# Experts' outputs transposed, from gated and split silu values, with all weights split ahead by GpSimd

## The reference, cut to what matters

```python
x = x + tanh(g_xattn) * attention(layernorm(x), ctx)      # 16 heads of 64, causal: the first 56 keys count
xf = layernorm(x).reshape(448, 128)
gates = softmax(xf @ router_w)                            # 14 routed experts, the best 2 kept
masked = gates of the best 2 / (their sum + 1e-9)
h_e = rmsnorm(xf) * rms_w[e]                              # per expert
routed = sum over e of masked[:, e] * (silu(h_e @ W1[e]) @ W2[e])   # W1 128x256, W2 256x128
shared = sum over 2 shared experts of silu(h @ W1) @ W2
x = x + tanh(g_ffn) * (routed + shared)
```

## Time and profile before

| what | us |
|---|---|
| median of 3 runs | 117.86 (117.8 to 119.21) |
| the profiled execution, its own time | 117.94 |
| its span (first to last instruction) | 116.1 |
| PE busy | 107.2 (92%) |
| PE weight loads busy | 91.6 (79%) |
| DVE busy | 69.3 (60%) |
| ACT busy | 59.4 (51%) |
| POOL busy | 43.8 (38%) |

### The profile page before, as it was taken

The page is one execution under the profiler, slowest core; times in us unless marked ns, Lnnn a source line. Parts: engine busy times, 40 slices in busy tenths (PEclk is TensorE's granted clock), DMA queues, the critical chain, the costliest instruction groups (busy, mean ns, idle before and its releaser), DMA issues.

```text
span 116.1 us, 2394 instructions
## 1 busy us (share of the span) xinstructions
PE 107.2 (92%) x826; PEld 91.6 (79%) x826; DVE 69.3 (60%) x195; ACT 59.4 (51%) x99; POOL 43.8 (38%) x75
## 2 busy tenths in 40 slices
PE   6699999996999999999699999999999999999980
PEld 6687768745496487488489989999999999999970
DVE  0068966659688789879843329999333333333360
ACT  5053787943579579579964298333333333333300
POOL 7803599000001000100101798666666666663000
PEclk9999999999999999999999999999999999999999
DMA  3899999999997000000000000000000000000003
GB/s 90 254 295 285 416 413 413 420 420 444 421 428 308 28 0 0 0 6 0 0 0 6 0 6 0 3 3 0 0 6 0 0 0 0 0 0 0 0 0 79
DMA packets 3169, 13.76 MB, mean 119 GB/s; under 512 B 431, under 2 KB 1007, under 8 KB 2775
## 3 DMA queue, kind: packets, MB, share of 16 engines
q1 hardware_dynamic: 3159, 13.63, 31.3%
HBM read 13.40 MB, written 0.23 MB: 117 GB/s over the span
## 4 chain that ended last, share of the span: by engine, by line
PE 57%; DVE 14%; DMA 12%; ACT 8%; SPq 4%; issue 3%; DVEq 0%; ACTq 0%
PE score_ps L736 15%; DMA ctx_all<-in_ctx_dram 12%; PE attn_ps L736 8%; PE ring L729 6%; PE ring L731 6%; PE ring L730 6%; PE ring L597 5%; ACT square_junk L816 4%; PE score_ps L552 4%; PE attn_ps L621 3%; DVE probs L1046 3%; DVE row_sum L1039 2%; DVE row_max L1025 2%; DVE probs L1032 2%; PE score_ps L546 2%
## 5 line engine op out<-in xcount | busy, mean ns | idle before, releaser
L938 ACT ACTIVATE mixT<-ring 128x896 f32<-128x896 f32 x16 | 14.6, 917 | 26.9 <-PE ring L731 26.9
L736 PE MATMUL score_ps<-w,mixT 128*112 (+1 forms) x160 | 19.1, 273 | 0.2 <-ACT mixT L938 0.2
L736 PEld LDWEIGHTS score_ps<-w,mixT 128*112 128x112 f32 x160 | 18.7, 177 | 0.8 <-issue 0.3
L437 POOL TENSOR_TENSOR h_scale<-h_base,minus_half 112x1 f32<-112x1 f32 x4 | 2.2, 547 | 41.7 <-DVE h_base L1069 41.7
L1210 DVE SCALAR_TENSOR_TENSOR xn_rows<-score_ps,gates,xn_rows 112x128 f32<-112x128 f32 x36 | 10.1, 343 | 11.5 <-PE score_ps L736 11.3
L621 PEld LDWEIGHTS attn_ps<-wkq_space,mixT 128*112 128x112 f32 x128 | 14.2, 177 | 2.4 <-issue 2.4
L621 PE MATMUL attn_ps<-wkq_space,mixT 128*112 128x128 f32 x128 | 15.0, 276 | 0.0
L402 POOL TENSOR_TENSOR w_full<-w,columns 128x256 f32 (+1 forms) x16 | 9.8, 612 | 11.5 <-PE ring L731 10.5
L729 PE MATMUL ring<-hT_hi,w_hi 128*128 128x448 f32 (+2 forms) x36 | 13.9, 386 | 0.1
L731 PE MATMUL ring<-hT_hi,w_lo 128*128 128x448 f32 (+2 forms) x36 | 12.6, 350 | 0.0
L730 PE MATMUL ring<-hT_lo,w_hi 128*128 128x448 f32 (+2 forms) x36 | 12.6, 349 | 0.0
(11 more groups left out here) (136 smaller groups left out, 186.7 us busy)
## 6 DMA issues: line engine op xcount, KB each, us to landing
ctx_all<-in_ctx_dram SPq DMA_DIRECT2D x4, 1500.0 KB, 18.8
w<-in_w_dram SPq DMA_DIRECT2D x2, 1792.0 KB, 27.3
wkq_space<-in_wkq_dram SPq DMA_DIRECT2D x2, 512.0 KB, 6.1
wvo<-in_wvo_dram SPq DMA_DIRECT2D x1, 1024.0 KB, 10.6
w<-in_w_shared_dram SPq DMA_DIRECT2D x2, 256.0 KB, 16.4
ctx_head<-in_ctx_head_dram SPq DMA_DIRECT2D x1, 480.0 KB, 8.9
ctx_headT<-in_ctx_headT_dram SPq DMA_DIRECT2D x1, 224.0 KB, 4.9
x_space<-in_x_rows_dram SPq DMA_DIRECT2D x1, 224.0 KB, 5.7
```

The source lines that it names most:

```text
L736: last = nc.tensor.matmul(dst, hidden[slot][:, c, t * ROWS:(t + 1) * ROWS], w2_chunk(c), start=(c == 0), stop=(c == 1))
L938: nc.scalar.activation(hidden[slot], ring[:, 2 * slot:2 * slot + 2, 0:TOKENS], ACT.Silu).then_inc(S["hidden_ready"], 1)
```

## The change

Outputs of experts are made with tokens along the columns (128 x 448), in one PSUM bank that sums over all experts, `out_sums`. So a gate is no longer one number per partition: DVE multiplies the hidden values (2 x 448 columns) by a tile that holds the gate of each token in all 128 rows (`gate_hidden`). The tiles of the first three routed experts are made by PE (`spread_gates`) from the transposed gates, split in hi and lo; those of the other eleven go through DRAM and come back by DMA, spread over the partitions. Experts 0 to 3 are multiplied by W2 in plain float32 (`output_whole`, two products of 448 columns); 4 to 15 from split values (`output_parted`, six fp32r products): ACT rounds the gated values (`round_hidden`), DVE subtracts (`subtract_hidden`). The shared experts' W2 is multiplied by tanh(g) beforehand. The loop is written out, and PE runs up to 5 experts ahead with the hidden products. The last expert is summed apart, in two halves of columns, and added by DVE; the result leaves transposed, in two DMAs, and is turned back on the host.

POOL splits all of W1, and W2 of experts 4 to 15, into places that hold them for good, most of it in the attention stage, with the four `second_scale` steps (the former L437) between. To make room, weights are loaded in fours into buffers that the attention has done with (`stages`), the context has room for two loads instead of four, and SP waits on semaphores between its loads. POOL also builds the matrix that spreads the gates.

```diff
+WHOLE = [0, 1, 2, 3]
+PARTED = [e for e in range(EXPERTS) if e not in WHOLE]
+FULL_SLOTS = 8
...
+GATE_GROUPS = [(3, 4), (4, 5), (5, 7), (7, ROUTED)]
+GATE_ROWS = 32
+CTX_SLOTS = 4
+AHEAD = 6
...
+        w1_hi, w1_lo = (sb(n, [P, EXPERTS, HIDDEN], FP32R) for n in ("w1_hi", "w1_lo"))
+        w2_hi, w2_lo = (sb(n, [P, len(PARTED), 2, D], FP32R) for n in ("w2_hi", "w2_lo"))
+        w2_whole = sb("w2_whole", [P, len(WHOLE), 2, D])
...
+        hidden_slots = key_space.rearrange("p (s c n) -> p s c n", s=FULL_SLOTS, c=2)
+        hi_slots = (parts(A_hi[:, :, :].rearrange("p h d -> p (h d)"), 2)
+                    + parts(ctx_hi_space, 1) + parts(probs_hi_space, 1))
+        lo_slots = (parts(A_lo[:, :, :].rearrange("p h d -> p (h d)"), 2)
+                    + parts(ctx_lo_space, 1) + parts(probs_lo_space, 1))
...
+                if 2 * n >= CTX_SLOTS:
+                    sp.wait_ge(S["squares_done"], GROUPS + 2 * n + 2 - CTX_SLOTS)
...
+            context(0)
+            context(1)
+            sp.dma_start(w2_whole[:, 0:SHARED, :, :], A["w2_shared"]).then_inc(S["w2_shared_loaded"], 16)
+            sp.dma_start(w2_whole[:, SHARED:, :, :], A["w2"][:, 0:len(WHOLE) - SHARED, :, :])\
+                .then_inc(S["w2_whole_loaded"], 16)
+            sp.wait_ge(S["ctx_lo_ready"], 1)
+            first_four(0)
+            sp.wait_ge(S["w1_scaled_ready"], SHARED)
+            sp.dma_start(stage_pair[:, :], A["w1"][:, 6 - SHARED:8 - SHARED, :].rearrange("p e f -> p (e f)"))\
+                .then_inc(S["w1_pair_loaded"], 16)
+            wait_filled(sp, "M3")
+            first_four(1)
+            first_four(2)
+            context(2)
+            sp.wait_ge(S["w1_scaled_ready"], 6)
+            second_four(0)
+            context(3)
+            sp.wait_ge(S["w1_scaled_ready"], 12)
+            second_four(1)
+            sp.wait_ge(S["w1_scaled_ready"], EXPERTS)
+            second_four(2)
+            sp.wait_ge(S["gatesT_ready"], 1)
+            sp.dma_start(gates_dram, gatesT).then_inc(S["gates_stored"], 16)
+            sp.wait_ge(S["gates_stored"], 16)
+            for n, (a, z) in enumerate(GATE_GROUPS):
+                sp.dma_start(gate_tiles[:, a - SPREAD:z - SPREAD, :], gates_dram[a:z, :].partition_broadcast(P))\
+                    .then_inc(gates_loaded[n], 16)
...
-                    .then_inc(S["w1_hi_ready"], 1)
-                pool.wait_ge(S["w1_hi_ready"], e + 1)
-                pool.wait_ge(S["w1_full_ready"], e + 1)
-                nc.gpsimd.tensor_tensor(w1_lo[slot][:, :], w1_full[:, :],
-                                        w1_hi[slot][:, :].bitcast(FP32), ALU.subtract)\
-                    .then_inc(S["w1_scaled_ready"], 1)
-            def scale_w1_static(e):
...
+                    nc.gpsimd.tensor_tensor(w1_full[:, :], first_weights(e),
+                                            rms_cols[:, e:e + 1].to_broadcast([P, HIDDEN]), ALU.mult)\
+                        .then_inc(S["w1_full_ready"], 1)
+                    pool.wait_ge(S["w1_full_ready"], e + 1)
+                    nc.gpsimd.tensor_copy(w1_hi[:, e, :], w1_full[:, :])\
+                        .then_inc(S["w1_hi_ready"], 1)
+                    pool.wait_ge(S["w1_hi_ready"], e + 1)
+                    nc.gpsimd.tensor_tensor(w1_lo[:, e, :], w1_full[:, :],
+                                            w1_hi[:, e, :].bitcast(FP32), ALU.subtract)\
+                        .then_inc(S["w1_scaled_ready"], 1)
...
+                    nc.gpsimd.tensor_copy(w2_hi[:, n, :, :], weights)\
+                        .then_inc(S["w2_hi_ready"], 1)
+                    pool.wait_ge(S["w2_hi_ready"], n + 1)
+                    nc.gpsimd.tensor_tensor(w2_lo[:, n, :, :], weights,
+                                            w2_hi[:, n, :, :].bitcast(FP32), ALU.subtract)\
+                        .then_inc(S["w2_split_ready"], 1)
...
+            split_w1(range(6))
...
+            split_w1(range(6, 12))
+            second_scale(0)
+            split_w1(range(12, EXPERTS))
+            second_scale(1)
+            split_w2(range(4, 8))
+            pool.wait_ge(S["tanh_ready"], 1)
+            pool.wait_ge(S["w2_shared_loaded"], 16)
+            nc.gpsimd.tensor_tensor(w2_whole[:, 0:SHARED, :, :], w2_whole[:, 0:SHARED, :, :],
+                                    tanh_col[:, 1:2].unsqueeze(2).unsqueeze(3)
+                                    .to_broadcast([P, SHARED, 2, D]), ALU.mult)\
+                .then_inc(S["w2_shared_scaled"], 1)
+            second_scale(2)
+            split_w2(range(8, 12))
+            second_scale(PAIRS - 1)
...
+            pool.wait_ge(S["logits_ready"], 1)
+            split_w2(range(12, 14))
+            pool.wait_ge(S["gatesT_ready"], 1)
+            split_w2(range(14, EXPERTS))
...
+            def next_hidden(e):
+                pe.wait_ge(S["hidden_ready"], e - 1)
+                hidden_products(e).then_inc(S["hidden_filled"], 1)
+            def output_whole(e):
+                if e < SHARED:
+                    pe.wait_ge(S["w2_shared_scaled"], 1)
+                    pe.wait_ge(S["hidden_ready"], e + 1)
...
+                    pe.wait_ge(S["hidden_gated"], e - SHARED + 1)
                 for c in range(2):
-                    last = nc.tensor.matmul(dst, hidden[slot][:, c, t * ROWS:(t + 1) * ROWS],
-                                            w2_chunk(c), start=(c == 0), stop=(c == 1))
+                    last = nc.tensor.matmul(out_sums, w2_whole[:, WHOLE.index(e), c, :], hidden(e)[:, c, :],
+                                            start=(e == 0 and c == 0), stop=False)
+                last.then_inc(S["expert_done"], 1)
+            def output_parted(e, sums, cols=slice(0, TOKENS)):
+                n = PARTED.index(e)
+                hi, lo = (hidden_part(slots, e) for slots in (hi_slots, lo_slots))
+                pe.wait_ge(S["w2_split_ready"], n + 1)
+                pe.wait_ge(S["hidden_hi_ready"], n + 1)
+                alone = e == EXPERTS - 1
+                for c in range(2):
+                    nc.tensor.matmul(sums, w2_hi[:, n, c, :], hi[:, c, cols],
+                                     start=(alone and c == 0), stop=False)
+                    nc.tensor.matmul(sums, w2_lo[:, n, c, :], hi[:, c, cols],
+                                     start=False, stop=False)
+                pe.wait_ge(S["hidden_lo_ready"], n + 1)
+                for c in range(2):
+                    last = nc.tensor.matmul(sums, w2_hi[:, n, c, :], lo[:, c, cols],
...
+            next_hidden(2)
+            output_whole(0)
+            next_hidden(3)
+            output_whole(1)
...
+            next_hidden(4)
+            pe.wait_ge(S["gates_ready"], 1)
+            for t in range(PAIRS):
+                last = nc.tensor.transpose(gatesT_ps[:, t * ROWS:(t + 1) * ROWS], gates[:, t, :],
+                                           ident[0:ROWS, 0:ROWS])
+            last.then_inc(S["gatesT_filled"], 1)
+            next_hidden(5)
+            def spread_gates(n):
+                nc.tensor.matmul(gate_banks[n], spread[:, n, :], gates_parts, start=True, stop=True)\
...
+            for e in range(3, EXPERTS - 1):
+                if e in WHOLE:
+                    output_whole(e)
+                else:
+                    output_parted(e, out_sums).then_inc(S["expert_done"], 1)
+                if e + AHEAD - 1 < EXPERTS:
+                    next_hidden(e + AHEAD - 1)
+            for n, cols in enumerate(halves):
+                output_parted(EXPERTS - 1, last_sums[n], cols).then_inc(S["half_done"], 1)
...
+                n = PARTED.index(e)
+                act.wait_ge(S["hidden_gated"], e - SHARED + 1)
+                if n >= PART_SLOTS:
+                    act.wait_ge(S["expert_done"], PARTED[n - PART_SLOTS] + 1)
+                nc.scalar.activation(hidden_part(hi_slots, e), hidden(e), ACT.Copy)\
+                    .then_inc(S["hidden_hi_ready"], 1)
...
+            for e in range(2):
+                silu(e)
+            act.wait_ge(S["logits_ready"], 1)
+            nc.scalar.activation(expo[:, :, :], shifted[:, :, :], ACT.Exp)\
...
+            nc.scalar.activation(x1T, x1T_ps, ACT.Copy).then_inc(S["x1T_ready"], 1)
+            silu(4)
+            act.wait_ge(S["gatesT_filled"], 1)
+            nc.scalar.activation(gates_parts, gatesT_ps, ACT.Copy).then_inc(S["gates_hi_ready"], 1)
+            act.wait_ge(S["w2_split_ready"], 4)
+            nc.scalar.activation(gatesT, gatesT_ps[0:ROUTED, :], ACT.Copy)\
+                .then_inc(S["gatesT_ready"], 1)
+            for e in range(5, 8):
+                silu(e)
+            round_hidden(4)
+            for e in range(8, EXPERTS):
+                round_hidden(e - 3)
+                silu(e)
+            for e in range(EXPERTS - 3, EXPERTS):
+                round_hidden(e)
...
-            def add_expert(place, gate, before=moe):
-                for t in range(PAIRS):
-                    last = nc.vector.scalar_tensor_tensor(
```

(23 more changed lines are left out.)

313 lines of the change are left out of this document (161 added, 152 removed).

## The result

The changed kernel takes 121.29 us (median of 4 runs, 120.56 to 122.08), the kernel before 117.83 beside it: a ratio of 1.029, 95% interval 1.020 to 1.038. It is slower. The profiled execution took 121.75 us, with a span of 119.9 against 116.1.

The account below looks back on a forecast made before the run. PE alone was taken to bound the expert stage, and a tight DVE, PE and ACT chain the attention stage. 117.94 - 5.1 (expert stage and end) + 8.4 (late POOL) = 121.2 us; range 116.5 to 124.5.

Parts of the forecast that it names:

- case A: Attention stage: POOL is late at h_scale and held up by DVE too; 121.2 us, range 119.5 to 123; chance 0.48.
- POOL's start after the load: POOL, attention stage: the next four experts' weights land at 25.6 us; from there POOL runs without a break.
- An expert's W1: POOL, attention stage: splitting one expert's W1 takes 1.9 us, with a copy put at 0.33.
- The spreading matrix: POOL, attention stage: memset, two selects and a copy take 2.2 us with waits, bounds 1.6 and 3.5.
- POOL's loss to DVE: Attention stage: POOL loses 0.5 us to each of seven L1046 instructions, 3.5 us up to the third h_scale.
- The waits are not to be added up: DVE's waits for h_scale: the third comes at 61.8 us when POOL's work is done, whatever DVE loses before.
- The loss by the clock after the first gap goes into the second wait: PE, attention stage: a clock fall after the first h_scale gap is absorbed by the wait at the third.
- C: Rival, attention stage: case A plus PE's clock falling in gaps ahead of h_scale, 2.5 us more, 123.7; chance 0.18.
- The fourth `h_scale` is covered: POOL, attention stage: it comes 4 x 1.1 + 0.6 us behind the third and is wanted about 7 us after it.
- The expert stage: From first expert output to last product: 39.3 us instead of 44.4, plus 1.0 charged for DVE; net gain 5.1.
- The end: After PE's last product: one DVE add of 224 columns, some 0.5 us with its wait; 1.05 less; output transfer unchanged.
- D: Rival, attention stage: POOL keeps up with DVE at h_scale, only the stage gain is left; 112.8 us; chance 0.10.

Follow-up runs that it names:

- inverse_in_psum: Changed kernel with the softmax inverse (row_inv) kept in PSUM and the idle products between the first transposes left out: 119.61 us, ratio 1.012.
- first_scale_early: Changed kernel with only POOL's first h_scale moved ahead of experts 9 to 11 of W1: 122.9 us, ratio 1.036.
- gap_products: Changed kernel with 5.7 us of W2 work moved behind the third h_scale (124.71 us), plus 30 idle PE products ahead of the last tile's transpose: 120.92 us.
- act_order: Changed kernel with ACT rounding expert e-2 instead of e-3 ahead of silu(e) from expert 12 on: 119.58 us, ratio 1.010.
- psum_weights: Changed kernel with W1 of experts 2 to 5 loaded ahead of the second context load and the softmax inverse in PSUM, POOL's order untouched: 115.07 us.

## Why the prediction was right

The forecast of 121.2 met 121.29, by case A. Its mechanism is the one that the runs show: POOL's work in front of the third `h_scale`, counted from the landing of the load, and the lock. That the number was met within 0.1 is in part luck, since errors of size cancelled:

- *POOL's start after the load*, 25.6: it was 26.11. *An expert's W1*, 1.9: it was 1.96 where another expert's follows and 1.84 where something else does (copy 0.40 for the 0.33 that I took). *The spreading matrix*, 2.2: 2.27 without the lock, 2.74 with it, inside the bounds. *W2*, 1.1: 1.15. *The shared W2*, 1.15: 1.00. *An `h_scale`*, 0.6: 0.54. Together these put the third step 0.9 us too early.
- *POOL's loss to DVE*, 3.5: `inverse_in_psum` puts it at 2.3. It was oversized: an L1234 cost POOL 0.26 to 0.45, not 0.5. DVE's own loss, put at 2 us, was 0.7 (eight times 717 less 625 ns). The errors of 0.9 and 1.2 nearly cancel: the third `h_scale`, forecast for 65.3, ended at 65.04, and the last `attention_out`, forecast for 66.9, started at 66.57.
- *The waits are not to be added up*: confirmed by `first_scale_early`.
- *The loss by the clock after the first gap goes into the second wait*: the clock did fall, to 0.52, which I had named as a sign of C. PE's half rate is part of the 2.88 us that DVE's `row_max` waited; the third `h_scale` still came last, by 1.37 us. So C's event happened without C's price, as this step had it, but with little to spare. It also took that PE kept its full clock through the third gap: in `inverse_in_psum` and `first_scale_early` it fell there, and the last `attention_out` took 5.32 us instead of 4.1. That the price is real where nothing hides it, 2.4 us, `gap_products` shows. The Trainium skill (TensorE: Matmul & The Clock Gate, "What's actually happening") has an idle PE fall to 1.2 GHz; the windows above agree, with 0.05 of 4 us busy ahead of a clock of 0.52.
- *The fourth `h_scale` is covered*: right for this order. POOL stood idle for 2.07 us ahead of it, the cover of 2 that follows from what I wrote (7 less 5), and DVE waited 0.66 there as in the kernel before. The cover is small: moving 5.7 us of work there lost 3.4 us.
- *The expert stage*: forecast 39.3 + 1.0 = 40.3 from this place, measured 41.8. The step that failed is "ACT has a silu and a rounding ... hidden". By amount of work it is, 0.92 + 0.95 in a beat of 2.48; but in its order a rounding stands behind a silu that PE has not fed yet, and at the end nothing is left to cover that. `act_order` gives 1.1 of the 1.5 back; the cause of the other 0.4 stays open. The other sizes held: DVE's pass 1.09 for 1.10, spread tiles by 85.7 where 77.2 + 8.1 = 85.3 was forecast, DVE held for 0.60 by the gates' way through DRAM and for 1.56 by ACT's first rounding, where about 2 was forecast for both.
- *The end*: DVE's part gave 1.15 instead of 1.05, and the output, left as it was in the forecast, gave 0.5. In sum the forecast had + 3.3 for the time and the profiled execution has + 3.8.

D, at 0.10, is nearly what `psum_weights` shows, with the order untouched: a span of 112.6, where D's 112.8 less the 1.84 around a span is 111.0. I had priced the copies and the matrix as what could bring D about; the load's place in SP's queue, 4.1 us, was the larger lever.
